# Edge-sum gathers of a graph network: GpSimd waits for the landing of every second group

## The chip, the cores and the metric

The kernel is one launch on one core of a Trainium2 chip. The metric is the device time of that launch in microseconds; lower is better. Three runs of the kernel before took 5539.73, 5543.76 and 5559.55 us, so its median is 5543.76 us.

## The reference

The reference runs eight layers over one graph of 3125 nodes (256 numbers each) and 50,000 edges sorted by destination: four graph layers, each followed by a layer of routed experts. Every layer adds its result to the node rows `x`. Three of the graph layers end in a sum over edges of this kind:

```
h   = project(norm(x))                        # one row of 256 a node
msg = h[src] * w_edge                         # one row an edge
agg = segment_sum(msg, dst, num_segments=n)   # one row a node
```

They differ in `w_edge`: a relation's matrix and an edge weight in the first graph layer, attention weights of eight heads in the third, a learned filter and a cutoff in the fourth. The second graph layer has such a sum too, but another function of the kernel computes it.

## The kernel before

The function `edge_sums` (line 540) is called three times, at lines 476 (`first=True`), 528 (`heads=8`) and 543 (`cut=...`). The text below calls them the first, second and third edge-sum stage. The edges stand in 416 blocks of 128 (`BLK`), padded so that all edges of a block belong to one tile of 125 nodes. Four blocks (`G`) are a group, so there are 104 groups (`NGB`).

For each block GpSimd issues one indirect DMA (line 607), a gather that fetches 128 rows from a table in device memory into `msg`. The tile `msg` holds six groups (`R = 6`), group `g` in buffer `g % 6`. Each buffer has its own semaphore `msg_in[g % R]`, to which a gather adds 16 when its rows have landed. From group 6 on, line 606 makes GpSimd wait, before each gather, until TensorE has finished the matmul that read the same place six groups earlier (semaphore `mm`).

The other engines work group by group as well:

- TensorE (`sums`, line 621) multiplies a matrix `same`, which says which of the 125 nodes an edge of the block belongs to, with `msg`, one product a block into `ps` (line 631). In the first stage it waits for `msg_in` itself; in the other two it waits for VectorE's `ready`. The first stage also counts edges on TensorE (`count`, line 638), and the second fetches the targets' attention numbers (line 618).
- ScalarE makes `same` (lines 703 to 713), or in the first stage the matrix for the count (lines 673 and 678); in the third stage it also copies the filters into PSUM (line 718).
- VectorE adds each product into the node rows (line 775). Before that it multiplies the gathered rows with the attention weights (lines 752 to 758, second stage) or the filters (line 764, third stage), which are the instructions that wait for `msg_in` there. In the first stage it makes `same` (line 743).
- SyncE loads one filter group of 512 KB for every group of the third stage, on a DMA queue of its own (line 596).

Each engine runs its own list of instructions in the order in which it is written. GpSimd's list in these stages is the gathers alone, with their waits:

```python
for j in range(G):
    n = g * G + j
    if g >= R:
        pool.wait_ge(mm, n - R * G + 1)
    nc.gpsimd.indirect_dma_start(msg[:, g % R, j, :], ...).then_inc(msg_in[g % R], 16)
```

Other indirect DMAs of GpSimd appear in the argument: the scatter of edge records in the opening (line 253), the gathers of the second graph layer (line 888, and line 878 between them) and those of a small edge sum (line 3120). The change does not touch them.

Of the kernel before, what the change touches and what calls it, by code (L numbers as in the profile page):

```python
# [20 lines left out]
G = 4  # L21
# [518 lines left out]
def edge_sums(k, table, idx, acc, heads=0, vt=None, cut=None, first=False, ramp_r=None):  # L540
# [10 lines left out]
    R = 6  # L551
    CH, CB = NGB // 8, BLK // 8
    with stage(k) as s:
# [3 lines left out]
        msg_in = [s.sem(f"msg_in{b}") for b in range(R)]  # L557
# [25 lines left out]
        with s.block() as block:  # L583
            @block.sync
            def _(sp):
                if first:
                    fields = k.rec.rearrange("(n p) f -> p n f", p=128)
                    with nc.allow_non_contiguous_dma(reason="four numbers an edge"):
                        for q in range(8):
                            sp.dma_start(raw[:, q * CB:(q + 1) * CB, :], fields[:, q * CB:(q + 1) * CB, D:RW]).then_inc(read, 16)  # L590
                            sp.wait_ge(read, 16 * q + 16)
                if cut is not None:
                    for g in range(NGB):
                        if g >= R:
                            sp.wait_ge(fil_ps, g - R + 1)
                        sp.dma_start(fil[:, g % R, :, :], k.rec[g * G * 128:(g + 1) * G * 128, 0:D].rearrange("(j p) f -> p j f", p=128)).then_inc(fil_in[g % R], 16)

            @block.gpsimd
            def _(pool):
                for g in range(NGB):  # L600
                    if first and g % CH == 0:
                        pool.wait_ge(known, g // CH + 1)
                    for j in range(G):
                        n = g * G + j
                        if g >= R:
                            pool.wait_ge(mm, n - R * G + 1)
                        nc.gpsimd.indirect_dma_start(msg[:, g % R, j, :], None, table, bass.IndirectOffsetOnAxis(idx[:, n:n + 1], 0)).then_inc(msg_in[g % R], 16)  # L607

            @block.tensor
            def _(pe):  # L610
                def targets(g):
                    pe.wait_ge(pick_done, g + 1)
                    if g >= 2:
                        pe.wait_ge(both_done, g - 1)
                    _, tiles = nc.values_load_multi_w_load_instructions(k.tile_i[0:1, g * G:(g + 1) * G], [mybir.EngineType.PE], min_val=0, max_val=NT - 1,
                                                                        skip_runtime_bounds_check_because="made as a count of at most 24")
                    for j, t in enumerate(tiles):
                        ins = nc.tensor.matmul(ps_v[:, g % 2, j * H2:(j + 1) * H2], pick[0:P, g % 2, j * 128:(j + 1) * 128], vt[:, ds(t, 1), :].rearrange("p t h -> p (t h)"), start=True, stop=True)
                    ins.then_inc(v_mm, 1)
# [101 lines left out]
            def _(dve):  # L721
# [44 lines left out]
                def sums(g):  # L766
                    _, tiles = nc.values_load_multi_w_load_instructions(k.tile_i[0:1, g * G:(g + 1) * G], [mybir.EngineType.DVE], min_val=0, max_val=NT - 1,
                                                                        skip_runtime_bounds_check_because="made as a count of at most 24")
                    for j, t in enumerate(tiles):
                        n = g * G + j  # L770
                        dve.wait_ge(mm, n + 1)
                        if n:
                            dve.wait_ge(added, n)
                        into = acc[:, ds(t, 1), :].rearrange("p t f -> p (t f)")
                        nc.vector.tensor_tensor(into, into, ps[:, j, 0:width], ALU.add).then_inc(added, 1)  # L775
# [2663 lines left out]
def build(nc, a, out, layers=8):  # L3439
# [3 lines left out]
    with ctx:  # L3443
# [30 lines left out]
        with nc.sbuf_tensor("src_rel", [128, BLK], I32) as src_rel, nc.sbuf_tensor("ramp_r", [128, P], F32) as ramp_r:  # L3474
            opening(k, a, x_rows, ramp_r)
            edge_sums(k, k.rel_rows.rearrange("n (r f) -> (n r) f", r=REL), src_rel, k.x, first=True, ramp_r=ramp_r)
# [46 lines left out]
        if layers >= 5:  # L3523
            vt8 = keep("vt8", [P, NT, 16])
            with sbt("rows_j") as rows, sbt("cols_j", [128, 2, N]) as cols, sbt("proj_j", [P, NT, D + 16]) as proj:
                head(k, rows, cols, proj, a["gat2_w"], D, d["gat8"], 8, a["gat2_a1"], a["gat2_a2"], vt=vt8, src_out=tiles("gat8")[:, :, D:D + 16], fetch=(answered, wt))
            with sbt("agg_j", [P, NT, D + 8]) as agg, sbt("out_j") as o:
                edge_sums(k, d["gat8"], k.src_i, agg, heads=8, vt=vt8)
                divide(k, agg, o, 8, 0.0)
                add_to_x(k, o)  # L3530
# [6 lines left out]
        if layers >= 7:  # L3537
            with sbt("rows_l") as rows, sbt("cols_l", [128, 2, N]) as cols, sbt("proj_l") as proj:
                head(k, rows, cols, proj, a["L3_gnn_lin1_w"], D, d["lin1"])
            with sbt("agg_m") as agg:  # L3540
                with sbt("cut", [128, BLK]) as cut, sbt("minus_cut", [128, BLK]) as minus_cut:
                    cutoff(k, cut, minus_cut)
                    edge_sums(k, d["lin1"], k.src_i, agg, cut=(cut, minus_cut))
                two_linears(k, agg, a["L3_gnn_lin2_w"], a["L3_gnn_lin2_b"], a["L3_gnn_lin_w"], a["L3_gnn_lin_b"])
# [53 lines left out]
```

## Time and profile before

| what | value |
|---|---|
| median of three runs | 5543.76 us |
| profiled execution, from first to last instruction | 6173.2 us |
| GpSimd busy, whole span | 3072.9 us (50%) |
| TensorE busy, whole span | 4074.4 us (66%) |
| gathers of line 607 | 3 stages of 416, 946 ns median each |

The profile is of one execution, which took longer than each of the three timed runs. Its span is the only time of that execution that is given. An indirect DMA on GpSimd is shown as busy while its descriptors are made, not while its rows travel. Where a wait is put down to a transfer of an earlier stage (such as `rows_g<-d_xn` or `rel_rows<-row`), the semaphore's number had belonged to that transfer before; the wait then ended with a semaphore of the stage at hand.

### The profile page before, as it was taken

Reading aid. Unit: us, or ns where it says so; the run is one execution under the profiler, and the core shown is the slowest. Engines: PE = TensorE matmul, PEld = TensorE weight load, DVE = VectorE, ACT = ScalarE, POOL = GpSimd, SP = SyncE. Lnnn points to the kernel's source line nnn. Section 1 sums busy time; section 2 is a strip of 40 time slices with the busy share of each in tenths; the row PEclk is TensorE's granted clock in tenths of the full one; section 3 lists DMA queues with packets and bytes.
Section 4 is the critical chain, followed back from the end, with each engine's and each line's share of the span. In section 5 each row is a group of like instructions: output and inputs, shape, how many; then the busy total and the mean of one; then the engine's idle time right before and its main releaser. Section 6 shows DMA issues by size and latency. Waiting matters only on the chain. (4 is left out here: it accounts for less than half of the span.)

```text
span 6173.2 us, 66416 instructions
## 1 busy us (share of the span) xinstructions
PE 4074.4 (66%) x17366; PEld 2897.1 (47%) x17366; DVE 3273.6 (53%) x7095; ACT 2796.0 (45%) x6254; POOL 3072.9 (50%) x3130
## 2 busy tenths in 40 slices
PE   7888555567837777256485776857776774555665
PEld 4555333347824445222264444835555662223465
DVE  6444355456555566699634665255556125444532
ACT  4777333322335566466343442335553213666532
POOL 3666566633446566267414552436662323666333
PEclk8999777768957887699796887967776886777888
DMA  4444533355643333355502223543333324566356
GB/s 129 150 150 148 114 90 91 90 124 180 174 115 91 94 96 95 72 167 166 135 1 61 47 43 104 179 118 95 95 95 70 118 63 129 179 181 181 81 159 203
DMA packets 442553, 721.00 MB, mean 117 GB/s; under 512 B 150695, under 2 KB 322521, under 8 KB 437660
## 3 DMA queue, kind: packets, MB, share of 16 engines
q1 hardware_dynamic: 299057, 374.14, 21.6%
q0 software_dynamic: 139600, 337.72, 20.1%
q10 hardware_dynamic: 3530, 4.89, 0.2%
q8 instruction: 152, 2.49, 0.2%
q14 instruction: 214, 1.75, 0.1%
HBM read 565.71 MB, written 153.73 MB: 117 GB/s over the span
## 5 line engine op out<-in xcount | busy, mean ns | idle before, releaser
L631 PE MATMUL ps<-msg,same 128*125 128x256 f32 (+1 forms) x2496 | 953.6, 524 | 671.2 <-issue 269.6
L631 PEld LDWEIGHTS ps<-msg,same 128*125 128x125 f32 x2496 | 566.1, 251 | 986.6 <-issue 574.2
L888 POOL DMA_INDIRECT msg<-d_gat,src_i x416 | 406.0, 976 | 266.9 <-PE ps L949 137.8
L253 POOL DMA_INDIRECT rec<-rec,slot_i x391 | 379.7, 971 | 304.4 <-DVE rec L431 133.6
L607 POOL DMA_INDIRECT msg<-d_lin,src_i x416 | 393.2, 945 | 275.0 <-issue 101.9
L607 POOL DMA_INDIRECT msg<-rel_rows,src_rel x416 | 399.0, 959 | 223.1 <-issue 95.4
L607 POOL DMA_INDIRECT msg<-d_gat,src_i x416 | 393.5, 946 | 226.3 <-PE ps L631 90.7
L949 PE MATMUL ps<-msg,same 128*125 128x260 f32 x832 | 300.5, 495 | 175.9 <-DVE agg_c L1111 130.9
L278 PE MATMUL ps_f<-w,hs 128*128 128x256 f32 x1568 | 383.6, 398 | 48.9 <-DVE rec L431 30.4
L278 PEld LDWEIGHTS ps_f<-w,hs 128*128 128x128 f32 x1568 | 298.8, 196 | 156.9 <-issue 61.3
L2962 PE MATMUL ps_y<-pr,ident 128*128 128x447 f32 (+1 forms) x448 | 209.3, 593 | 238.3 <-DVE pr L3044 238.3
L2032 ACT ACTIVATE hid<-ps_h,w 128x128 f32<-128x128 f32 x572 | 207.4, 367 | 325.9 <-PE ps_h L1983 206.1
L3120 POOL DMA_INDIRECT msg<-d_small,idx x256 | 241.8, 945 | 162.6 <-DVE weighed L3223 88.7
L1983 PE MATMUL ps_h<-xT,w 128*128 128x128 f32 x2288 | 292.0, 280 | 11.3 <-DMA w<-in_L_ffn_packed 8.4
L3137 PE MATMUL ps<-spread,oh_lo 128*125 128x500 f32 x512 | 255.1, 658 | 66.8 <-DVE spread L3229 66.8
L1983 PEld LDWEIGHTS ps_h<-xT,w 128*128 128x128 f32 x2288 | 284.1, 196 | 21.4 <-DMA w<-in_L_ffn_packed 9.2
L949 PEld LDWEIGHTS ps<-msg,same 128*125 128x125 f32 x832 | 176.1, 234 | 251.2 <-DVE agg_c L1111 163.1
L2930 POOL TENSOR_TENSOR dB<-rows,u 128x894 f32<-128x894 f32 (+1 forms) x112 | 215.1, 1922 | 153.9 <-DMA rows<-bc_d 145.8
L775 DVE TENSOR_TENSOR x<-x,ps 125x256 f32 x416 | 174.7, 420 | 216.8 <-DMA w_rel<-in_w_rel 95.2
L775 DVE TENSOR_TENSOR agg_m<-agg_m,ps 125x256 f32 x416 | 174.7, 420 | 211.3 <-DMA got<-answered,slot_i 128.5
L775 DVE TENSOR_TENSOR agg_j<-agg_j,ps 125x264 f32 x416 | 178.1, 428 | 188.3 <-PE ps L631 87.9
L713 ACT ACTIVATE same<-off,cut,minus_cut 128x125 f32<-128x125 f32 x416 | 170.4, 481 | 226.7 <-DMA got<-answered,slot_i 164.0
(632 smaller groups left out, 9885.5 us busy)
## 6 DMA issues: line engine op xcount, KB each, us to landing
w<-in_L_ffn_packed SPq DMA_DIRECT2D x170, 514.0 KB
fil<-rec SPq DMA_DIRECT2D x104, 512.0 KB
rows<-bc_d SPq DMA_DIRECT2D x96, 447.0 KB
rel_rows<-row SPq DMA_DIRECT2D x25, 896.0 KB
got<-answered SPq DMA_DIRECT2D x30, 560.0 KB
ahead<-in_L_ffn_packed SPq DMA_DIRECT2D x8, 2052.0 KB
lo_rows<-ffn_lo_r SPq DMA_DIRECT2D x32, 500.0 KB
msg<-d_gat,src_i POOLq DMA_INDIRECT x832
```

Source lines behind the costliest of these rows:

```text
L253: nc.gpsimd.indirect_dma_start(k.rec, bass.IndirectOffsetOnAxis(slot_i[0:some_rows, c:c + 1], 0), rec[0:some_rows, g % R, j, :], None).the ...
L278: ins = nc.tensor.matmul(ps_f[:, v % 2, i, :], hs[:, (2 * g + c) % 4, j * 128:(j + 1) * 128], w2[:, c, :], start=c == 0, stop=c == 1)
L607: nc.gpsimd.indirect_dma_start(msg[:, g % R, j, :], None, table, bass.IndirectOffsetOnAxis(idx[:, n:n + 1], 0)).then_inc(msg_in[g % R], 16)
L631: nc.tensor.matmul(ps[:, j, 0:width], same[:, g % 2, j, :], msg[:, g % R, j, 0:width], start=True, stop=True).then_inc(mm, 1)
L775: nc.vector.tensor_tensor(into, into, ps[:, j, 0:width], ALU.add).then_inc(added, 1)
L888: nc.gpsimd.indirect_dma_start(msg[:, g % R, j, :], None, table, bass.IndirectOffsetOnAxis(idx[:, n:n + 1], 0)).then_inc(msg_in[g % R], 16)
L949: nc.tensor.matmul(ps[:, n % 3, 0:width], same[:, g % 2, j, :], msg[:, g % R, j, 0:width], start=True, stop=True).then_inc(mm, 1)
L1983: ins = nc.tensor.matmul(ps_h[:, at % 4, 0:BR], part(n, c * x.f + f * 128, 128), xT[:, n % 2, c, :], start=c == 0, stop=c == 1)
L2930: ins = nc.gpsimd.tensor_tensor(into, both(rows[:, n % R, 0, 0:hi - lo], hi - lo), u[:, :, lo:hi], ALU.mult)
L2962: ins = nc.tensor.matmul(ps_y[:, h, 0:size(n)], k.ident[:], pr[:, n % 2, h * size(n):(h + 1) * size(n)], start=st == 0, stop=st == SN - 1)
L3120: nc.gpsimd.indirect_dma_start(msg[:, g % R, j, :], None, table, bass.IndirectOffsetOnAxis(idx[:, n:n + 1], 0)).then_inc(msg_in[g % R], 16)
L3137: nc.tensor.matmul(ps[:, 0:NT * W], oh_lo[:, g % 2, j, :], spread[:, g % 2, j, :], start=False, stop=False).then_inc(mm, 1)
```

## The change

After the four gathers of every group with an odd number, GpSimd waits until all four have landed, before it goes on to the next group. The bound of the wait is the one with which the consumers wait for that group.

```diff
@@ -605,6 +605,8 @@
                         if g >= R:
                             pool.wait_ge(mm, n - R * G + 1)
                         nc.gpsimd.indirect_dma_start(msg[:, g % R, j, :], None, table, bass.IndirectOffsetOnAxis(idx[:, n:n + 1], 0)).then_inc(msg_in[g % R], 16)
+                    if g % 2 == 1:
+                        pool.wait_ge(msg_in[g % R], 16 * G * (g // R + 1))
 
             @block.tensor
             def _(pe):
```

## Rows read from the trace of the kernel before

**Rows 1.** The page's head and its busy times of the engines.
```profile
span 6173.2 us, 66416 instructions
PE 4074.4 (66%) x17366; PEld 2897.1 (47%) x17366; DVE 3273.6 (53%) x7095; ACT 2796.0 (45%) x6254; POOL 3072.9 (50%) x3130
```

**Rows 2.** Indirect DMAs by line: count, duration ns min/median/max, first and last start.
```profile
L253 POOL DMA_INDIRECT rec<-rec,slot_i x391: 929/971/1158, 84.8 to 691.0; - x196
L607 POOL DMA_INDIRECT msg<-rel_rows,src_rel x416: 940/946/1241, 709.6 to 1313.1; - x139
L888 POOL DMA_INDIRECT msg<-d_gat,src_i x416: 940/946/1438, 1794.6 to 2504.0; - x139
L878 POOL DMA_INDIRECT got<-d_xn,order_i x25: 1191/1195/1541, 1799.9 to 2309.8; - x25
L3120 POOL DMA_INDIRECT msg<-d_small,idx x256: 939/944/1187, 3294.2 to 3697.5; - x128
L607 POOL DMA_INDIRECT msg<-d_gat,src_i x416: 940/946/1190, 4082.6 to 4694.4; - x139
L607 POOL DMA_INDIRECT msg<-d_lin,src_i x416: 940/946/973, 5167.8 to 5765.7; - x139
```

**Rows 3.** Busy us by stretch: PE, PEld, DVE, ACT, POOL; clock, DMA share, GB/s.
```profile
709.00:1314.00 605.00, 324.65 (x1183) 220.50 (x1184) 296.20 (x987) 188.08 (x499) 399.03 (x416) 0.71 0.38 91
4082.00:4696.00 614.00, 429.64 (x1693) 321.86 (x1693) 333.92 (x789) 307.83 (x696) 393.51 (x416) 0.76 0.36 95
5167.00:5767.00 600.00, 312.60 (x792) 175.15 (x792) 284.18 (x493) 375.43 (x904) 393.23 (x416) 0.73 0.62 181
5168.00:5183.00 15.00, 3.78 (x8) 2.50 (x8) 7.25 (x3) 7.97 (x20) 11.35 (x13) 0.50 1.04 338
```

**Rows 4.** GpSimd in order of time, first stage: start, us, instruction, [idle before <-releaser].
```profile
913.17 0.95 POOL L607 DMA_INDIRECT msg<-rel_rows,src_rel  x1 [0.30 <-issue]
914.42 0.95 POOL L607 DMA_INDIRECT msg<-rel_rows,src_rel  x1 [0.30 <-issue]
917.96 0.94 POOL L607 DMA_INDIRECT msg<-rel_rows,src_rel  x1 [2.58 <-DMA w_rel<-in_w_rel]
```

**Rows 5.** TensorE, VectorE and ScalarE in order of time, same stretch.
```profile
910.47 0.35 PE L638 MATMUL ps_n<-hot_t,hot_r 128*125 128x25 bf16 x4
918.40 0.76 PE L631 MATMUL ps<-msg,same 128*125 128x256 f32 x1 [7.58 <-DVE x L775]
915.63 1.11 DVE L743 TENSOR_SCALAR same<-ramp_r,lo,edge_w 128x125 f32<-128x125 f32 x4 [5.75 <-DMA rel_rows<-row]
915.62 0.62 ACT L678 ACTIVATE hot_r<-gap 128x500 bf16<-128x500 f32 x1 [8.22 <-DMA rel_rows<-row]
```

**Rows 6.** Second stage in order of time: one gather after each of three pauses, and TensorE and VectorE between.
```profile
4140.25 0.96 POOL L607 DMA_INDIRECT msg<-d_gat,src_i  x1 [2.10 <-PE ps L631]
4146.56 0.96 PE L618 MATMUL ps_v<-vt,pick 125*128 x8
4151.79 0.22 DVE L752 TENSOR_TENSOR both<-msg,ps_v 128x64 f32<-128x64 f32 x1 [1.67 <-DMA rows_g<-d_xn]
4152.10 0.96 POOL L607 DMA_INDIRECT msg<-d_gat,src_i  x1 [1.34 <-PE ps L631]
4163.93 0.95 POOL L607 DMA_INDIRECT msg<-d_gat,src_i  x1 [2.04 <-PE ps L631]
```

**Rows 7.** GpSimd in order of time elsewhere: direct and indirect DMAs.
```profile
4817.73 2.19 POOL L2130 DMA_DIRECT2D answered<-zero  x4
4820.22 1.30 POOL L2122 DMA_INDIRECT rows<-tokens,token_i  x1 [0.30 <-issue]
```

**Rows 8.** Start of the second stage: last gathers of groups 0 and 1, and their first readers.
```profile
4086.63 0.94 POOL L607 DMA_INDIRECT msg<-d_gat,src_i  x1 [0.30 <-issue]
4091.63 0.94 POOL L607 DMA_INDIRECT msg<-d_gat,src_i  x1 [0.30 <-issue]
4089.53 0.22 DVE L752 TENSOR_TENSOR both<-msg,ps_v 128x64 f32<-128x64 f32 x1 [0.63 <-DMA msg<-d_gat,src_i]
4094.52 0.22 DVE L752 TENSOR_TENSOR both<-msg,ps_v 128x64 f32<-128x64 f32 x1 [3.17 <-DMA msg<-d_gat,src_i]
```

**Rows 9.** Start of the third stage: last gather of group 1 and its first reader.
```profile
5176.55 0.94 POOL L607 DMA_INDIRECT msg<-d_lin,src_i  x1 [0.30 <-issue]
5182.36 1.22 DVE L764 TENSOR_TENSOR msg<-msg,ps_f 128x1024 f32<-128x1024 f32 x1 [3.23 <-DMA msg<-d_lin,src_i]
```

## Prediction

> **What bounds the kernel now.** I read the page's head first. No engine is busy for more than 66% of the span [rows 1], so the whole has no single bound. The change touches three stages, so each stage is read by itself.
>
> The list by line gives the length of the stages from the first to the last start of their 416 gathers [rows 2]: 603.5, 611.8 and 597.9 us. Per group of four that is 5.80, 5.88 and 5.75 us. The table by stretch then says which engine could need that long [rows 3]. Divided by 104 groups, the busiest consumer is TensorE with 4.1 us in the second stage and ScalarE with 3.6 us in the third; VectorE has at most 3.2 us. GpSimd is next. A gather is busy for 0.95 us and the next one starts 0.30 us later even when nothing holds it, so the pitch is 1.25 us [rows 4] and a group needs 5.0 us. That is more than any consumer's work, and the DMA engines are a third busy in two of the stages [rows 3]. GpSimd's pitch is therefore the floor of these stages: 415 x 1.25 = 518.8 us.
>
> In this profile the stages lie 85, 93 and 79 us above the floor, and order of time shows why. GpSimd runs a dozen gathers at the pitch, of which the rows show the last two, and then stands for 2.58 us instead of 0.30 [rows 4]. In the same stretch TensorE's last matmul ends at 910.8 and the next starts at 918.4, while VectorE and ScalarE, which wait for TensorE's counts, both start at 915.6 [rows 5]. So a finished matmul was known to the others some 5 us late. The second stage repeats this every two groups: GpSimd's pauses end at 4140.25, 4152.10 and 4163.93, and VectorE gets the product of 4146.56 (ended 4147.5) only at 4151.79, with GpSimd standing [rows 6]. The buffers fill up, GpSimd stops, the late signals arrive, and all go on.
>
> **Is that so in the timed runs?** The profiled execution took 629.4 us more than the median, so something in it is stretched. I take the six stages in which GpSimd issues indirect DMAs one behind the other and subtract 1.25 us for each interval from their length [rows 2]: 606.2 - 390 x 1.25 = 118.7 (line 253); 84.7, 93.0 and 79.1 (line 607); 709.4 - 440 x 1.25 = 159.4 (lines 888 and 878 together); 403.3 - 255 x 1.25 = 84.5 (line 3120). The sum is 619.4 us, which is almost the whole difference. The likeliest reading is that the late signals belong to the profiled execution and that the timed runs go at the gathers' pitch there, about 520 us a stage. The 0.30 us between gathers looks like part of the indirect form, not of the recording: four direct DMAs of GpSimd take 2.19 us together without a gap, and the indirect one behind them again starts 0.30 us after [rows 7].
>
> **The change, part by part.** It removes nothing and moves no transfer to another queue. It adds 52 waits in each stage, 156 in all. Behind the waiting instruction on GpSimd stand the eight gathers of the next two groups and nothing else; TensorE (first stage) or VectorE (the others) waits for their rows. SyncE's filter loads go on unhindered. The 52nd wait stands behind the last gather and delays no other, so 51 count in each stage, 153 in all.
>
> *Price of one wait.* The trace has no wait of GpSimd for its own gather. The nearest rows are consumers that stood idle for a landing. Group 0 of the second stage: last gather over at 4086.63 + 0.94 = 4087.57, reader starts at 4089.53, 1.96 us later; group 1: 4092.57 to 4094.52, 1.95 us [rows 8]. This includes landing, signal and start of the reader, which GpSimd pays as well. The next gather so starts 1.95 us after the last one's end instead of 0.30: 1.65 us a wait. From below, the price is zero where GpSimd would have stood anyway, and it could be below zero if the pause lets other engines' signals through earlier. From above, the third stage's start has 5182.36 - (5176.55 + 0.94) = 4.87 us [rows 9], thus 4.57 a wait, but the filter loads then fill all DMA engines (share 1.04), against 0.62 over that stage [rows 3]. I take 1.65 for all three stages: 0.62 is no full queue, and what the third costs more goes into the range.
>
> The Trainium skill speaks against the change: "DMA: Bandwidth & Descriptors", section "Rules for kernel authors", says to issue a transfer early and to wait for its semaphore late, since the fixed cost then overlaps. Its section "Anatomy of one DMA" gives about 2.0 us for that fixed cost on GpSimd's path; as an estimate, 153 such waits would come to 306 us. The 1.95 us of the rows agrees with it, and the sum below goes by the rows.
>
> *Cover.* With one wait, two groups cost GpSimd 7 x 1.25 + 0.95 + 1.95 = 11.65 us, a stage 52 x 11.65 = 606 us. Against the floor of about 520 us this is 153 x 1.65 = 252 us in all, uncovered, since no consumer needs as long. Against the profiled stages (603.5, 611.8, 597.9) it is 606 x 3 - 1813 = +5 us: there the waits fall into pauses that exist anyway. So on the profile's own time I expect a span near 6173 + 5 = 6178 if the waits take the pauses' place and up to 6425 if they come on top, and on the timed median 5543.8 + 252 = **5796 us**.
>
> **The rivals.**
> *Same pauses in the timed runs.* If the late signals are there too, the waits replace them, by the sum above +5 us: 5549. For it: the second stage already pauses every second group, as the change would have it [rows 6]. Against it: the 629 us then have no place in the profile. Also here: the rows have already landed when the wait comes, so that it holds nothing; the 1.95 us speak against that [rows 8].
> *The wait is cheaper than the pause it replaces (faster).* If the pauses are real and the rows land sooner without recording, a regular stop lets TensorE's signals through before the buffers are full. It decides where the stop is under 1.95 us; each 0.1 us less gives 153 x 0.1 = 15 us. At 1.45 us, half a microsecond less: 153 x 0.5 = 77, less the 5 above: 5472. For it: signals came with GpSimd standing [rows 5, 6]. Against: it needs both conditions.
> *Half the slack is real.* Timed stages of about 560 us cover half the cost: 126 us, 5670.
> *The filters fill the queue.* The third stage pays 4.57 us a wait: 51 x 2.92 = 149 us more, 5945.
>
> **How the numbers follow.** My forecast has a chance of 0.60, with its own range of 5700 to 5870; half the slack 0.07; full queue 0.03; same pauses 0.18; cheaper stop 0.12. A change of 0.5% (28 us) is about what a measurement of this kernel can tell from none. Slower is 0.60 + 0.07 + 0.03 = 0.70, same 0.18, faster 0.12. The range runs from 5500, which takes in the even case, to 5870, the forecast with some 70 us for the third stage; the 5472 and 5945 cases, 0.15 together, stay out.
>
> **What would show it.** In the changed profile every eighth gather should stand about 1.95 us behind the one before, released by its own landing, 51 times a stage; some 2.3 us or more in the third would be the filters. Stages of about 606 us confirm the cycle. If the profile's span hardly moves while the timed median rises by 200 us or more, the late signals were the recording's. If both stay, they were real. I am wrong if the gathers' pitch falls below 1.25 us, if the pauses of 2 us and more come on top of the waits, or if the timed median falls.

## The result: 324 us slower

Four runs of the changed kernel have a median of 5876.07 us (5868.5 to 5896.77), four of the kernel before 5551.66 us. The ratio is 1.0608, with a 95% interval of 1.0591 to 1.0625. The forecast had the sign and the mechanism, but 5796 us and an upper end of 5870 us; the measured median lies 6 us above that end.

The profile of the changed kernel comes first. The first line has the span, the others are the indirect DMAs by line (count, duration in ns min/median/max, first and last start). They answer to [rows 1, 2]; lines behind 607 have moved by two, so that line 888 is now 890 and line 3120 is 3122.

```profile
core 0 of [0], span 5875.0 us
L253 POOL DMA_INDIRECT rec<-rec,slot_i x391: 929/971/1224, 82.3 to 603.4; - x196
L607 POOL DMA_INDIRECT msg<-rel_rows,src_rel x416: 940/946/1223, 622.0 to 1254.0; - x139
L890 POOL DMA_INDIRECT msg<-d_gat,src_i x416: 940/946/1427, 1721.3 to 2300.4; - x139
L3122 POOL DMA_INDIRECT msg<-d_small,idx x256: 940/944/1187, 3082.0 to 3400.6; - x128
L607 POOL DMA_INDIRECT msg<-d_gat,src_i x416: 940/946/1190, 3764.1 to 4385.9; - x139
L607 POOL DMA_INDIRECT msg<-d_lin,src_i x416: 940/946/980, 4848.0 to 5499.8; - x139
```

Two things are to be seen. The three edge-sum stages take 632.0, 621.8 and 651.8 us, above the 606 us that I had reckoned for each. And this execution is not stretched as the first one was: its span of 5875.0 us is its timed 5876.72 us but for 1.7 us, and the stages that the change does not touch are much shorter than in [rows 2]. The small edge sum (line 3122) takes 318.6 us, which is 255 intervals of 1.25 us, where it took 403.3.

GpSimd in order of time shows the added waits (start, us, instruction, [idle before and what ended it]). These are the last gather of group 1 and the gathers behind the first four waits of the second stage.

```profile
3773.07 0.95 POOL L607 DMA_INDIRECT msg<-d_gat,src_i  x1 [0.30 <-issue]
3776.12 0.94 POOL L607 DMA_INDIRECT msg<-d_gat,src_i  x1 [2.10 <-DMA msg<-d_gat,src_i]
...
3787.80 0.94 POOL L607 DMA_INDIRECT msg<-d_gat,src_i  x1 [1.99 <-PE ps L633]
...
3800.68 0.94 POOL L607 DMA_INDIRECT msg<-d_gat,src_i  x1 [3.18 <-DMA msg<-d_gat,src_i]
...
3813.12 0.94 POOL L607 DMA_INDIRECT msg<-d_gat,src_i  x1 [2.75 <-DMA msg<-d_gat,src_i]
```

Every eighth gather stands, as forecast, until the gathers before it have landed. Where the profile names TensorE, a signal of it that GpSimd also waits for came at about the same time: in the trace's semaphore records the last signal of the landing lies 0.26 us ahead of the next gather in all 153 stops. The shortest stop, 1.99 us, is near the 1.95 us that I had read from two readers [rows 8], but many are longer: 2.1, 2.75, 3.18. The mean of the 51 stops is 2.35 us in the first stage, 2.31 in the second and 2.90 in the third; the middle one is 2.12, 2.13 and 2.89 us. Three stops in a row of the third stage:

```profile
5000.52 0.95 POOL L607 DMA_INDIRECT msg<-d_lin,src_i  x1 [3.16 <-PE ps L633]
...
5012.78 0.94 POOL L607 DMA_INDIRECT msg<-d_lin,src_i  x1 [2.57 <-DMA msg<-d_lin,src_i]
...
5025.70 0.94 POOL L607 DMA_INDIRECT msg<-d_lin,src_i  x1 [3.22 <-DMA msg<-d_lin,src_i]
```

### The profile page after: what moved, and what is told of

Its sections match the earlier page's. It is cut to its first block and busy times, and to the rows that moved or that the text cites. A ratio compares the mean times of both kernels' runs of the same rounds, so it can differ in the third digit from the quotient of the medians.

```text
span 5875.0 us, 66563 instructions
## 1 busy us (share of the span) xinstructions
PE 4045.5 (69%) x17366; PEld 2972.3 (51%) x17366; DVE 3282.5 (56%) x7095; ACT 2801.8 (48%) x6254; POOL 3072.4 (52%) x3130
## 5 line engine op out<-in xcount | busy, mean ns | idle before, releaser
L633 PE MATMUL ps<-msg,same 128*125 128x256 f32 (+1 forms) x2496 | 1035.1, 579 | 769.2 <-DVE agg_m L777 308.8
L633 PEld LDWEIGHTS ps<-msg,same 128*125 128x125 f32 x2496 | 665.9, 285 | 1056.1 <-DVE msg L766 386.7
L278 PE MATMUL ps_f<-w,hs 128*128 128x256 f32 x1568 | 367.5, 388 | 8.4 <-DVE hs L422 8.0
L951 PE MATMUL ps<-msg,same 128*125 128x260 f32 x832 | 272.5, 462 | 93.7 <-DVE agg_c L1113 93.5
L766 DVE TENSOR_TENSOR msg<-msg,ps_f 128x1024 f32<-128x1024 f32 x104 | 127.0, 1221 | 296.6 <-DMA msg<-d_lin,src_i 278.6
L680 ACT ACTIVATE hot_r<-gap 128x500 bf16<-128x500 f32 x104 | 64.4, 619 | 428.0 <-PE ps_n L640 424.6
L2964 PEld LDWEIGHTS ps_y<-pr,ident 128*128 128x128 f32 x448 | 82.1, 202 | 360.4 <-DVE pr L3046 210.6
L2072 DVE TENSOR_TENSOR y<-ps_o,b 128x256 f32<-128x256 f32 (+1 forms) x202 | 85.8, 425 | 316.5 <-PE ps_o L2010 243.7
```

The lines of the kernel that those rows point to most:

```text
L278: ins = nc.tensor.matmul(ps_f[:, v % 2, i, :], hs[:, (2 * g + c) % 4, j * 128:(j + 1) * 128], w2[:, c, :], start=c == 0, stop=c == 1)
L633: nc.tensor.matmul(ps[:, j, 0:width], same[:, g % 2, j, :], msg[:, g % R, j, 0:width], start=True, stop=True).then_inc(mm, 1)
L951: nc.tensor.matmul(ps[:, n % 3, 0:width], same[:, g % 2, j, :], msg[:, g % R, j, 0:width], start=True, stop=True).then_inc(mm, 1)
L2964: ins = nc.tensor.matmul(ps_y[:, h, 0:size(n)], k.ident[:], pr[:, n % 2, h * size(n):(h + 1) * size(n)], start=st == 0, stop=st == SN - 1)
```

## The experiments

Theory L is that the change costs what GpSimd stands until the rows have landed, because without it the stages go at the gathers' pitch. The rivals are named where they are tested.

**The kernel before once more.** No edit; a second profile.

> The kernel before, unchanged, for a second profile. Theory L (the change costs what GpSimd stands until the rows have landed, and without it the stages go at the gathers' pitch of 1.25 us): a profile whose span is near the timed 5550 us, with the three stages 520 to 535 us long each and no signal of TensorE later than 1 us. Rival P (the long pauses of the first profile are part of every execution): stages of 600 us and more in a profile whose span is near 5550 us too.

Measured: 5539.01 us. Its span, its indirect DMAs by line, and behind line 607 the only two waits that it has inside the stages (us in total, times); then the three stages by stretch, with columns as in [rows 3]:

```profile
core 0 of [0], span 5537.2 us
L253 POOL DMA_INDIRECT rec<-rec,slot_i x391: 930/974/1162, 80.9 to 601.3; - x196
...
L607 POOL DMA_INDIRECT msg<-rel_rows,src_rel x416: 942/949/1201, 619.9 to 1143.0; - x139
L607 POOL DMA_INDIRECT msg<-d_gat,src_i x416: 942/949/1192, 3657.1 to 4177.1; - x139
L607 POOL DMA_INDIRECT msg<-d_lin,src_i x416: 942/949/982, 4642.7 to 5162.4; - x139
  issue: 279.8, 918
  PE ps L631: 99.7, 327
...
L888 POOL DMA_INDIRECT msg<-d_gat,src_i x416: 941/949/1444, 1611.9 to 2187.1; - x139
L3120 POOL DMA_INDIRECT msg<-d_small,idx x256: 940/947/1187, 2971.1 to 3290.3; - x128
```
```profile
619.90:1144.00 524.10, 318.04 (x1224) 250.19 (x1224) 312.89 (x1026) 196.00 (x520) 397.50 (x416) 0.76 0.44 105
3657.00:4178.00 521.00, 437.81 (x1743) 304.66 (x1744) 347.56 (x813) 321.25 (x727) 394.42 (x416) 0.80 0.42 111
4642.00:5164.00 522.00, 313.37 (x816) 184.59 (x816) 290.87 (x508) 388.11 (x935) 394.16 (x416) 0.76 0.70 209
```

The stages are 523.1, 520.0 and 519.7 us long against a floor of 518.8. The 327 waits for TensorE come to 99.7 us, 0.30 us each: that is the gap that every gather has, so none of them held anything. The long pauses of [rows 4, 6] are gone, and rival P with them. The busiest consumer, TensorE in the second stage, has 437.81 / 104 = 4.2 us of work a group, against 5.0 us of GpSimd. The changed kernel's stages are longer than these by 108.9, 101.8 and 132.1 us, 342.8 in all; the two spans differ by 5875.0 - 5537.2 = 337.8 us. The same list of waits in the changed kernel:

```profile
  issue: 246.0, 805
  PE ps L633: 135.8, 305
  DMA msg<-d_lin,src_i: 124.0, 43
  DMA msg<-rel_rows,src_rel: 115.3, 49
  DMA msg<-d_gat,src_i: 98.7, 43
```

The gaps between its gathers come to 719.8 us, against 279.8 + 99.7 = 379.5 us in the kernel before. These 340.3 us are nearly all of the 342.8, so the stages grew by what GpSimd stood.

**One stage at a time.** In place of `if g % 2 == 1`:

```diff
+                    if first and g % 2 == 1:              # e2
+                    if att and g % 2 == 1:                # e3
+                    if cut is not None and g % 2 == 1:    # e4
```

> The waits in the first edge-sum stage alone. Theory L prices each by the changed kernel's profile: the gather behind a wait starts 2.35 us after the one before instead of 0.30, so 51 x 2.05 = 104 us, 5656 us. Rival S (the loss comes from one stage, the third, where the filters' loads share the DMA engines): under 40 us here.

> The waits in the second edge-sum stage alone. Theory L: 2.31 us instead of 0.30, 51 x 2.01 = 103 us, 5654 us. Rival S: under 40 us.

> The waits in the third edge-sum stage alone. Theory L: 2.90 us instead of 0.30, 51 x 2.60 = 133 us, 5684 us; the three stages' sums would then come to 340 us beside the measured 324. Rival S: 250 us or more of the 324 here.

| waits in | median us | ratio (95%) | more than before, us | expected by L |
|---|---|---|---|---|
| first stage | 5659.93 | 1.0214 (1.0187 to 1.0240) | 113 | 104 |
| second stage | 5644.28 | 1.0184 (1.0156 to 1.0213) | 98 | 103 |
| third stage | 5674.20 | 1.0228 (1.0201 to 1.0255) | 128 | 133 |

The kernel before had a median of 5546.69 us beside them. The three parts come to 338 us, so they add up to the whole change within the spread of the runs. Each stage pays for itself and the third pays most, but far from all: rival S is out. In each of the three profiles the other two stages stay at their floor; with the waits in the first alone:

```profile
L607 POOL DMA_INDIRECT msg<-rel_rows,src_rel x416: 940/946/1239, 623.8 to 1256.3; - x139
L607 POOL DMA_INDIRECT msg<-d_gat,src_i x416: 942/946/1191, 3767.6 to 4286.6; - x139
L607 POOL DMA_INDIRECT msg<-d_lin,src_i x416: 942/946/977, 4750.0 to 5268.8; - x139
...
  DMA msg<-rel_rows,src_rel: 121.0, 51
```

The last line counts the stops of the first stage: 51 of 121.0 / 51 = 2.37 us.

**A wait behind every group.** Against the changed kernel:

```diff
-                    if g % 2 == 1:
-                        pool.wait_ge(msg_in[g % R], 16 * G * (g // R + 1))
+                    pool.wait_ge(msg_in[g % R], 16 * G * (g // R + 1))
```

> A wait behind every group instead of every second one: 103 waits a stage with a gather behind them. Theory L: each costs what it cost in the changed kernel, 103 x (2.05 + 2.01 + 2.60) = 686 us, 6237 us. Rival D (the cost lies in the loss of lead: with few groups in flight the consumers run late, and that loss is there once): clearly less than twice the 324 us, say 400 us, 5950 us.

Measured: 6135.87 us, ratio 1.1058 (1.1032 to 1.1084), 591 us more than the 5545.29 us of the kernel before beside it. The cost does follow the number of waits, and rival D, which wanted some 400 us, is out. But twice the waits cost 591 / 324 = 1.8 times as much, not 2.1 times. The waits of line 607, us in total and times:

```profile
  DMA msg<-d_gat,src_i: 230.7, 103
  DMA msg<-d_lin,src_i: 229.4, 103
  DMA msg<-rel_rows,src_rel: 228.3, 103
```

The stops are 2.24, 2.23 and 2.22 us, the third stage's no longer than the others, though the filters are loaded as before. The traces show why: the loads come at another time. Here are the 2 us behind the last gather ahead of two stops of the third stage, first of the changed kernel (the stops that end at 5000.52 and 5012.78), then of this one (two stops of 2.08 and 2.06 us); the number before the last is the DMA engines' share:

```profile
4997.36:4999.36 2.00, 1.91 (x5) 1.51 (x6) 1.07 (x3) 0.00 (x0) 0.00 (x0) 0.50 0.91 322
5010.21:5012.21 2.00, 2.00 (x5) 1.63 (x6) 1.18 (x3) 0.00 (x0) 0.00 (x0) 0.50 0.75 272
```
```profile
5356.34:5358.34 2.00, 0.26 (x1) 0.00 (x0) 0.09 (x1) 1.64 (x5) 0.00 (x0) 0.79 0.25 80
5363.13:5365.13 2.00, 0.22 (x1) 0.00 (x0) 0.10 (x1) 1.68 (x5) 0.00 (x1) 0.78 0.26 80
```

Over all stops of the third stage this share has a mean of 0.83 in the changed kernel and of 0.31 here, where the changed kernel's stages without filters have 0.30. In the changed kernel a filter load runs while the rows land; with a wait behind every group it is over by then. L's price of 2.90 us for the third stage so did not hold here: 103 x (2.90 - 2.23) = 69 us of the 95 us by which 591 falls short of its 686.

**The wait one gather later.** The condition stands inside the loop over `j`, behind the first gather of the next group. Against the kernel before:

```diff
+                        if j == 0 and g and g % 2 == 0:
+                            pool.wait_ge(msg_in[(g - 1) % R], 16 * G * ((g - 1) // R + 1))
```

> The same waits, each one gather later: GpSimd issues the first gather of the next group and then waits for the odd group. Theory L: the gather issued in between covers 1.25 us of each stop, so the rest is 1.10, 1.06 and 1.65 us instead of 0.30, 51 x (0.80 + 0.76 + 1.35) = 148 us, 5700 us. Rival D: one gather more in flight changes the lead by an eighth, so nearly the whole 324 us stays, above 5820 us.

Measured: 5735.17 us, ratio 1.0336 (1.0312 to 1.0360), 190 us more than before. Its stages:

```profile
L607 POOL DMA_INDIRECT msg<-rel_rows,src_rel x416: 940/946/1213, 622.2 to 1189.1; - x139
L607 POOL DMA_INDIRECT msg<-d_gat,src_i x416: 940/946/1190, 3706.1 to 4264.8; - x139
L607 POOL DMA_INDIRECT msg<-d_lin,src_i x416: 940/946/980, 4728.0 to 5348.8; - x139
```

They are 566.9, 558.7 and 620.8 us long, so 44, 39 and 101 us above the undisturbed ones, where L expected 41, 39 and 69. In the first two stages the gather in between covers its 1.25 us of each stop, within 3 us a stage. In the third it saves 31 us where L expected 64, so L missed there: the filters' loads still meet the landing (the share of the 2 us behind the awaited gather has a mean of 0.78). Rival D, above 5820 us, is out here too.

**As many waits, each for the group before.** Against the kernel before:

```diff
+                    if g % 2 == 1:
+                        pool.wait_ge(msg_in[(g - 1) % R], 16 * G * ((g - 1) // R + 1))
```

> As many waits at the same places, but each for the group before the one just issued, whose rows have had 5 us to land. Theory L: no stop is left, 5552 us within half a per cent. Rival W (the waits as instructions cost something on GpSimd): 156 waits at 0.3 us, about 50 us more.

Measured: 5544.74 us, ratio 0.9998 (0.9985 to 1.0012).

```profile
L607 POOL DMA_INDIRECT msg<-rel_rows,src_rel x416: 942/946/1242, 622.3 to 1146.7; - x139
L607 POOL DMA_INDIRECT msg<-d_gat,src_i x416: 942/946/1190, 3664.2 to 4183.3; - x139
L607 POOL DMA_INDIRECT msg<-d_lin,src_i x416: 942/946/973, 4646.7 to 5165.6; - x139
```

The stages last 524.4, 519.1 and 518.9 us. A wait for rows that have had four more gathers' time, 5 us, costs nothing, and neither do the 156 instructions: rival W is out.

**Six groups of filters.** The changed kernel, with the loop of line 593 cut to the first six groups and its consumer's wait to match:

```diff
-                    for g in range(NGB):
+                    for g in range(R):
                         if g >= R:
                             sp.wait_ge(fil_ps, g - R + 1)
...
-                        act.wait_ge(fil_in[g % R], 16 * (g // R + 1))
+                        act.wait_ge(fil_in[g % R], 16)
```

> The changed kernel with only the first six groups of filters loaded in the third stage, which are then used again for all groups (so the loads of the other 98 groups are left out, and the filters of those groups are not theirs). Theory L with the filters' loads as the reason for the third stage's longer stop: 2.31 us instead of 2.90 there, 51 x 0.59 = 30 us less than the changed kernel, 5846 us. Rival T (the third stage's rows themselves land later): no less than the changed kernel's 5876 us and 2.9 us a stop.

Measured: 5851.29 us, ratio 1.0536 (1.0508 to 1.0565). Its three stages by line 607; behind them the third stage's stretch, first in this kernel and then in the changed one (columns as in [rows 3]):

```profile
L607 POOL DMA_INDIRECT msg<-rel_rows,src_rel x416: 941/949/1233, 623.7 to 1249.6; - x139
L607 POOL DMA_INDIRECT msg<-d_gat,src_i x416: 941/947/1191, 3778.8 to 4400.6; - x139
L607 POOL DMA_INDIRECT msg<-d_lin,src_i x416: 941/947/981, 4862.6 to 5481.4; - x139
```
```profile
4862.00:5482.00 620.00, 354.34 (x816) 221.61 (x816) 292.08 (x508) 389.30 (x936) 393.81 (x416) 0.65 0.32 93
```
```profile
4848.00:5501.00 653.00, 335.97 (x816) 213.55 (x816) 292.56 (x509) 388.67 (x935) 393.23 (x416) 0.70 0.56 167
```

Without the loads the third stage falls from 651.8 to 618.8 us, 33 us against the 30 expected, and is as long as the others; the DMA engines' share goes from 0.56 to 0.32. So the filters' loads make the third stage's rows land later, and rival T is out.

## Why the prediction was right in kind and too low

**The bound.** That GpSimd's pitch of 1.25 us sets these stages was right. The second profile of the same kernel has them at 520 to 523 us, and no other engine holds a gather there.

**The first profile.** I took its late signals of TensorE for something that the timed runs do not have, because the excess of six stages over the pitch (619.4 us) nearly made up the difference to the median (629.4 us). The second profile confirms that: 5537.2 us with no pauses. The sum matched better than it should have, though, which was luck: the six stages became 555 us shorter and not 619, since the scatters of line 253 (520.4 us) and the gathers of line 888 (575.2 us) stay some 30 us above the pitch also without late signals, and 81 of the 636 us between the two profiles lie outside the six. And I put the signals down to recording as such and expected the changed kernel's profile at 6178 us or, with the waits on top, up to 6425. It came out at 5875.0 us, the time of an unstretched execution. Of the ten profiles in this study only the first has the late signals. What disturbed that one execution stays open.

**The price of a wait: the step that failed.** I took 1.65 us for all 153 waits, from two readers at the start of the second stage [rows 8]. Measured by the lengths of the stages it was 108.9 / 51 = 2.13 us in the first, 101.8 / 51 = 2.00 in the second and 132.1 / 51 = 2.59 in the third. The missing 0.48, 0.35 and 0.94 us, times 51, are 90 us, and with my 252 they are the 343 us of the profiles. Three things were missing. First, I held that GpSimd pays what the reader pays, but it goes on later. Behind group 1 of the second stage VectorE starts, in the changed kernel too, 1.94 us after the last gather's end (3773.07 + 0.95 = 3774.02):

```profile
3775.96 0.22 DVE L754 TENSOR_TENSOR both<-msg,ps_v 128x64 f32<-128x64 f32 x1 [3.23 <-DMA msg<-d_gat,src_i]
```

GpSimd's next gather starts at 3776.12, 2.10 us after it. In the second and third stage GpSimd goes on 0.17 us behind VectorE in 99 of the 102 stops (0.26 us after the landing's last signal, where VectorE starts 0.09 us after it); for 153 waits that is 153 x 0.17 = 26 us. The two samples were thus typical landings: with the 0.17 us they give the middle stop of 2.12 us. Second, two samples could not show that some stops take 2.5 to 4.1 us, which lift the mean of the first two stages to 2.35 and 2.31 us: about 20 us. Third, I knew of the filters' loads in the third stage and bounded their effect by 4.57 us a wait, but gave it nothing in the sum and only some 70 us in the upper end, which then also had to hold the other stages' excess. The stops there have a mean of 2.90 us, about 40 us beyond the middle stop of the others, of which 33 us go with the loads. The three come to 86 of the 90 us. An upper end at the 5945 us that this bound gives would have held the time.

**The added waits and their cover.** That 51 waits count in each stage and that they add up is shown by the kernels with one stage each (113, 98 and 128 us) and by the wait behind every group. That nothing hides them is shown from the other side: one gather issued in between takes 1.25 us off each stop in the first two stages, four take everything. In the third stage the one gather took off less, for the loads.

**The rivals.** Pauses in the timed runs, a stop cheaper than the pause it replaces, and half the slack all fall with the second profile of the kernel before, in which the stages lie at most 4.3 us above the floor. The filters in the queue are real, but cost 33 us and not 149: a stop as long as in [rows 9] is only the first of the stage, 5.00 us.

**The estimate of 306 us.** From the Trainium skill, "DMA: Bandwidth & Descriptors", section "Anatomy of one DMA", I had estimated 306 us with its fixed cost of about 2.0 us. The profile's stops of 1.99 to 2.1 us agree with the figure, and the longer ones and those beside the filters' loads are what it does not cover. That the measured 324 is nearer to the 306 than to my own sum is luck: a stop takes the place of a gap of 0.30 us, which the estimate did not take off; with it off, the estimate from the same figure is 153 x 1.70 = 260 us. The rule of the Trainium skill to wait late, on the same page in the section "Rules for kernel authors", is what the wait for the group before shows: the same number of waits, at no cost.

**Still open.** Why some stops take 2.5 us and more in the first two stages, where no filters are loaded. The traces show that it is not chance, for the same groups have them: in all twelve stages with a wait for the group just issued, the stops behind groups 7, 15, 19, 23 and 31 took at least 2.50 us, and the one behind group 101 took 3.8 to 4.2. By the reference's edge list the last block of each of these five groups is mostly padding (91 to 123 of 128 places), and the last three blocks of group 101 are nothing else; a padded place fetches row 0 of the table (lines 726 and 727 of the kernel before, where its fields are 0). Perhaps a gather that asks for one row that often lands later; no run changed the padding. Other long stops of the second stage recur without it: those behind groups 5, 17, 29, 61, 73 and 85 took 2.7 to 3.4 us in each of the three profiles that wait there behind every second group.

## What to carry to other kernels

A wait on the engine that issues gathers cost the whole landing here, where that engine's issue rate was the stage's limit, and nothing when it asked for rows that were four issues old: place it one group behind. Price a landing by its mean over many stops and beside the transfers that share the DMA engines, not by one or two readers at a stage's start. When a profile's span differs from the timed runs by several per cent, find the stages that make up the difference and take a second profile before anything is priced in them.

## What the runs showed that I had not expected

One profiled execution of an unchanged kernel was 636 us longer than another (6173.2 against 5537.2 us), 555 us of it in the six stages where GpSimd issues indirect DMAs one behind the other, with TensorE's signals reaching the other engines several microseconds late [rows 5, 6].

VectorE's total wait for gathered rows in the second stage doubled with the change, by 97.5 us, which is nearly the whole 101.8 us by which the stage grew: the stop of GpSimd is seen a second time, as idle time of its reader. Here is the line of the kernel before (second profile) and of the changed one, each as total us, times and longest:

```profile
DVE both L752 <- DMA msg<-d_gat,src_i: 99.0, 100, 3.4
```
```profile
DVE both L754 <- DMA msg<-d_gat,src_i: 196.5, 98, 5.1
```
